# Layer 3's transposed h: TensorE transposes replaced by VectorE block transposes and 16 small DMAs

## The reference, cut to what matters

```python
# layer 0: attention, elu        p = softmax(where(adj > 0.5, leaky(Wh1 + Wh2.T), -9e15), axis=1)
#                                x += elu((p @ h) @ W0)
# layer 1: normalised graph      x += relu(An @ h @ W1 + bias)
# layer 2: plain graph           x += relu((adj @ h) @ W2) * mask
# layer 3 (the one changed):
deg = sum(adj, -1); agg = (adj @ h) / max(deg, 1e-6)
x   = x + relu(concat([h, agg]) @ W3.T)
```

## Time and profile before

| | us |
|---|---|
| median of 3 runs | 2621.51 (2621.48 to 2623.4) |
| the profiled execution's own time | 2621.74 |
| its span, first to last instruction | 2619.9 |
| mean granted TensorE clock | 0.992 of full speed |
| TensorE matmul busy | 2547.1 (97%) |
| VectorE busy | 1823.2 (70%) |
| ScalarE busy | 1408.7 (54%) |
| GpSimd busy | 1185.2 (45%) |

### The profile page before, as it was taken

How to read it: one execution, slowest core, us unless ns; L and a number is a source line. 1 busy time by engine, 2 the same in 40 slices (tenths; PEclk the granted TensorE clock), 3 DMA queues, 4 the chain that set the end, 5 groups by cost and what they waited for, 6 DMA issues and landing times.

```text
span 2619.9 us, 40393 instructions
## 1 busy us (share of the span) xinstructions
PE 2547.1 (97%) x13704; PEld 2205.5 (84%) x13704; DVE 1823.2 (70%) x4251; ACT 1408.7 (54%) x2571; POOL 1185.2 (45%) x1607
## 2 busy tenths in 40 slices
PE   2799999999999999999999999999999999999998
PEld 2688888888888888888888888888888888888886
DVE  6776676676676677677677777777776766766753
ACT  3555555555555555555555555555555555555542
POOL 2544444444444444444444444444444444444431
PEclk8899999999999999999999999999999999999999
DMA  4101111111011011011111111111111111111000
GB/s 140 41 29 49 33 41 49 33 41 49 30 44 49 29 45 49 29 45 46 33 45 41 37 45 41 37 45 35 42 46 33 41 49 33 41 49 33 29 17 25
DMA packets 72844, 109.30 MB, mean 42 GB/s; under 512 B 4288, under 2 KB 37056, under 8 KB 72640
## 3 DMA queue, kind: packets, MB, share of 16 engines
q1 hardware_dynamic: 72640, 106.71, 12.6%
HBM read 73.14 MB, written 33.55 MB: 41 GB/s over the span
## 4 chain that ended last, share of the span: by engine, by line
PE 96%; DVE 1%; issue 1%; ACT 1%; POOL 1%; DMA 0%; SPq 0%; POOLq 0%; ACTq 0%; DVEq 0%
PE O L277 46%; PE T L277 34%; PE X L277 13%; PE X L310 2%; PE X L298 1%; POOL h_lo L747 0%; ACT h L405 0%; DMA act_out<-w_all 0%; POOL xs L712 0%; DVE p_lo L589 0%; DVE scores L522 0%; DVE w_lo L512 0%; DVE t_lo L595 0%; ACT act_out L436 0%; DVE xs L630 0%
## 5 line engine op out<-in xcount | busy, mean ns | idle before, releaser
L747 POOL TENSOR_TENSOR h_lo<-h,h_hi 128x512 fp32r<-128x512 f32 x384 | 503.4, 1333 | 673.1 <-ACT h_hi L411 673.1
L595 DVE TENSOR_TENSOR t_lo<-T,t_hi 128x512 fp32r<-128x512 f32 x512 | 352.5, 690 | 399.1 <-ACT t_hi L417 399.1
L405 ACT ACTIVATE h<-xs,ln_bias,ln_scale 128x512 f32<-128x512 f32 x512 | 396.0, 811 | 391.9 <-POOL ln_bias L741 391.9
L277 PE MATMUL O<-w_hi,t_hi 128*128 128x512 f32 x1536 | 603.2, 393 | 0.0
L277 PE MATMUL O<-w_hi,t_lo 128*128 128x512 f32 x1536 | 598.2, 389 | 0.0
L277 PE MATMUL O<-w_lo,t_hi 128*128 128x512 f32 x1536 | 598.1, 389 | 0.0
L417 ACT CAST t_hi<-T 128x512 fp32r<-128x512 f32 x512 | 298.3, 584 | 257.1 <-PE T L277 257.1
L712 POOL TENSOR_TENSOR xs<-xs,act_out 128x512 f32<-128x512 f32 x128 | 163.7, 1297 | 531.7 <-ACT act_out L439 496.9
L277 PEld LDWEIGHTS O<-w_hi,t_lo 128*128 128x128 f32 x1536 | 288.3, 188 | 60.2
L277 PEld LDWEIGHTS O<-w_hi,t_hi 128*128 128x128 f32 x1536 | 288.5, 188 | 55.9 <-DVE t_lo L595 0.5
L277 PEld LDWEIGHTS O<-w_lo,t_hi 128*128 128x128 f32 x1536 | 288.6, 188 | 55.7
(11 more groups left out here) (92 smaller groups left out, 4991.4 us busy)
## 6 DMA issues: line engine op xcount, KB each, us to landing
xs<-x SPq DMA_DIRECT2D x64, 512.0 KB, 3.6
out<-xs SPq DMA_DIRECT2D x64, 512.0 KB, 2.8
a_raw<-adj_t SPq DMA_DIRECT2D x64, 256.0 KB, 2.7
a_rows<-adj SPq DMA_DIRECT2D x64, 256.0 KB, 2.7
xs<-w_all SPq DMA_DIRECT2D x6, 512.0 KB, 7.3
act_out<-w_all SPq DMA_DIRECT2D x2, 512.0 KB, 6.7
z<-w_all SPq DMA_DIRECT2D x2, 512.0 KB, 6.4
v_rows<-a_vecs SPq DMA_DIRECT2D x1, 512.0 KB, 5.4
```

What stands on the lines that cost most here:

```text
L277: last = nc.tensor.matmul(psum, s, m, start=(start and n == 0 and i == 0), stop=(stop and n == len(pairs) - 1 and i == 2))
L405: nc.scalar.activation(h[:, k.odd, m], xs[:, k.xb, m], ACT.Relu, bias=ln_bias[:, k.quad, m:m + 1], scale=ln_scale[:, k.quad, m:m + 1], acc ...
L595: nc.vector.tensor_tensor(t_lo[:, k.odd, c], T[:, c], t_hi[:, k.odd, c].bitcast(F32), ALU.subtract).then_inc(t_lo_ready, 1)
L747: nc.gpsimd.tensor_tensor(h_lo[:, k.odd, m], h[:, k.odd, m], h_hi[:, k.odd, m].bitcast(F32), ALU.subtract).then_inc(h_lo_ready, 1)
```

## The change

`transpose_h` and its PSUM results go. In slot 0, ahead of `mean_relu`, VectorE waits for layer 3's h and turns it with two transpose instructions (one for each 128 rows), which transpose every 32x32 block within its quadrant of 32 partitions, SBUF to SBUF, into `act_out[:, 1]`. SyncE waits for both, and then issues 16 DMAs, one for each pair of a source and a target quadrant, SBUF to SBUF, ahead of the store of that slot. Each moves 32 partitions x 256 values (32 KB): 1 KB in a row on the source side, eight runs of 32 values (128 bytes) on the target side. The target is the memory of `h[:, 1]` itself, which has been read by then. ScalarE casts it in one instruction to `ht_hi` once all 16 have landed, and VectorE subtracts in one instruction; both now read SBUF where they read PSUM before. ScalarE's next `activate` into `h[:, 1]` waits for that subtraction, `scaled_relu` for the moves.

```diff
+        turned = flat(act_out[:, 1]).rearrange("p (q b n) -> p q b n", q=QUADS, b=FT * NT)
+        turned_tiles = flat(act_out[:, 1]).rearrange("p (q c m n) -> p m c q n", q=QUADS, c=FT, m=NT)
+        h_blocks = h[:].rearrange("p b m (c q f) -> p b m c q f", c=FT, q=QUADS)
+        ht = [flat(h[:, odd]) for odd in range(2)]
+        ht_blocks = [t.rearrange("p (b q n) -> p b q n", q=QUADS, b=FT * NT) for t in ht]
+        MOVES = 16 * QUADS * QUADS
...
# SyncE
+            def move_blocks(k):
+                wait(sp, turned_ready, k.done(L3, NT))
+                for i in range(QUADS):
+                    for o in range(QUADS):
+                        sp.dma_start(ht_blocks[k.odd][QUAD * o:QUAD * o + QUAD, :, i],
+                                     turned[QUAD * i:QUAD * i + QUAD, o]).then_inc(ht_moved, 16)
...
                     load_x(old.g + X_BUFS)
+                if step(j + 3).layer == 3:
+                    move_blocks(step(j + 3))
                 over = step(j - 1)
# TensorE
-                wait(pe, ht_lo_ready, k.done(L3, NT, back=1))          (in spread)
-            def transpose_h(k):
-                wait(pe, h_ready, k.done(ALL, NT))
-                wait(pe, z_ready, k.done(L3, NT, back=4))
-                wait(pe, scores_ready, k.done(L0, NT, back=3))
-                for half in range(2):
-                    for f in range(HALF * half, HALF * half + HALF):
-                        for m in range(NT):
-                            c = (f % HALF) * N + m * P
-                            last = nc.tensor.transpose(X[:, half, c:c + P], h[:, k.odd, m, f * P:f * P + P], ident[:])
-                    last.then_inc(ht_psum_ready, 1)
-                if step(j + 2).layer == 3:
-                    transpose_h(step(j + 2))
# ScalarE
-                wait(act, ht_psum_ready, k.done(L3, NT, back=2))       (in activate)
+                wait(act, ht_lo_ready, k.done(L3, back=2))
             def transposed(k):
                 wait(act, z_psum_ready, k.done(L3, NT, back=4))
-                for half in range(2):
-                    wait(act, ht_psum_ready, k.part(L3, NT, half))
-                    nc.scalar.copy(ht_hi[:, HALF * half:HALF * half + HALF],
-                                   X[:, half].rearrange("p (f n) -> p f n", f=HALF)).then_inc(ht_hi_ready, 1)
+                wait(act, ht_moved, k.done(L3, MOVES))
+                nc.scalar.copy(flat(ht_hi[:]), ht[k.odd]).then_inc(ht_hi_ready, 1)
# VectorE
+            def turn(k):
+                wait(dve, h_ready, k.done(ALL, NT))
+                wait(dve, l1_done, k.done(L1, back=3))
+                for m in range(NT):
+                    nc.vector.transpose(turned_tiles[:, m], h_blocks[:, k.odd, m]).then_inc(turned_ready, 1)
             def transposed(k):
-                for half in range(2):
-                    c = slice(HALF * half, HALF * half + HALF)
-                    wait(dve, ht_hi_ready, k.part(L3, NT, half))
-                    nc.vector.tensor_tensor(ht_lo[:, c], X[:, half].rearrange("p (f n) -> p f n", f=HALF),
-                                            ht_hi[:, c].bitcast(F32), ALU.subtract).then_inc(ht_lo_ready, 1)
+                wait(dve, ht_hi_ready, k.done(L3))
+                nc.vector.tensor_tensor(flat(ht_lo[:]), ht[k.odd], flat(ht_hi[:]).bitcast(F32),
+                                        ALU.subtract).then_inc(ht_lo_ready, 1)
...
+                wait(dve, ht_moved, k.done(L3, MOVES, back=-2))        (in scaled_relu)
...
+                if step(j + 3).layer == 3:
+                    turn(step(j + 3))
                 if step(j - 1).layer == 3:
                     mean_relu(step(j - 1))
```

More of the change, by code:

```diff
@@ L12 @@
 P = 128
+QUAD = 32
+QUADS = P // QUAD
 LAYERS = 4
@@ L85, in sem, with flat @@
             return ctx.enter_context(nc.semaphore(name))
+        def flat(t):
+            return t.rearrange("p m n -> p (m n)")
         w_hi = sb("w_hi", [P, WEIGHTS, FT, F], F32R)
@@ L161, in gnn_kernel @@
         t_ready, o_ready = sem("t_ready"), sem("o_ready")
-        wh_rows_ready, ht_psum_ready, z_psum_ready = sem("wh_rows_ready"), sem("ht_psum_ready"), sem("z_psum_ready")
+        wh_rows_ready, z_psum_ready = sem("wh_rows_ready"), sem("z_psum_ready")
+        turned_ready, ht_moved = sem("turned_ready"), sem("ht_moved")
         stats_ready, mv_ready, neg_mean_ready, var_ready, rstd_ready, scale_ready, ln_ready = (
@@ L196, in tiles @@
             return dram[g].rearrange("(m p) f -> p m f", p=P)
-        def flat(t):
-            return t.rearrange("p m n -> p (m n)")
         def flat_blocks(t):
@@ L293, in spread @@
                 wait(pe, wh_ready, k.done(L0, DOTS))
-                wait(pe, ht_lo_ready, k.done(L3, NT, back=1))
                 wait(pe, scores_ready, k.done(L0, NT, back=4))
@@ L341, in project_first @@
                     wait(pe, w_lo_ready, 2 * WEIGHT_ORDER.index(4) + 2)
-                wait(pe, ht_lo_ready, k.done(L3, NT))
+                wait(pe, ht_lo_ready, k.done(L3))
                 for n in range(NT):
@@ L401, in activate @@
                 wait(act, wh_ready, k.done(L0, DOTS, back=2))
-                wait(act, ht_psum_ready, k.done(L3, NT, back=2))
+                wait(act, ht_lo_ready, k.done(L3, back=2))
                 for m in range(NT):
@@ L614, in scaled_relu @@
                 wait(dve, deg_rsqrt_ready, k.done(L0, back=SPACING))
+                wait(dve, ht_moved, k.done(L3, MOVES, back=-2))
                 for n in range(NT):
```

## The result

The changed kernel takes 2653.58 us (median of 4 runs, 2651.91 to 2655.87) against 2621.49 us: a ratio of 1.0122, 95% interval 1.0105 to 1.014. It is 32 us slower; I had forecast 27 us faster. The profiled execution has a span of 2654.1 us against 2619.9, 34.1 us more before rounding.

What follows compares the result with a forecast made beforehand. TensorE was taken to bound the kernel: -53.1 us for 61 graphs without transposes, +3.5, +10.2 and +10.3 for exposed ends, +2 for the clock, -27.1 on 2621.7, gave 2594.5 us; range 2580 to 2730.

Steps and rivals of the forecast that it cites:

- What bounds, and what is removed: TensorE bounds the steady part; removing its eight transposes of h saves 0.87 us in each of 61 graphs.
- Step 1: Layer 3's h is ready at 1316.88; VectorE waits 1.2 us for it at the head of its slot.
- Step 2: Two block transposes of 128x512 on VectorE take 0.65 us each, done at 1318.2.
- Step 3: SyncE, idle there, issues 16 DMAs 0.53 us apart; the last issue starts at 1326.2.
- rival B: ht_lo misses its place beside GpSimd, waits for the second h_lo, 0.7 us late per graph: 2639 us; chance 0.17.
- Step 4: The last DMA lands at 1328.9, with 13 ns estimated for a 128-byte piece, 57 ns at the upper end.
- rival A: Small DMA pieces are slower than the issues and set the pace: 2713 us at 45 ns a piece; chance 0.27.
- Step 8: TensorE wants ht_lo at 1332.3, leaving 0.6 us of cover; nothing is added to the period.
- Step 7: VectorE's ht_lo, 1.22 us with two SBUF sources, waits for GpSimd's h_lo until 1330.5 and ends at 1331.7.
- Step 6: VectorE's slot 0 moves by 2.5 us, but T is still free in time for TensorE, with 2.4 us of cover.
- The ends: New path exposed in the first graph, +3.5 us, and the last two, +10.2 and +10.3, plus 2 for the clock.
- My sign of being wrong: The prediction is wrong if TensorE waits for ht_lo in the steady part.

Runs made afterwards that it cites:

- experiment 2: Changed kernel, 16 moves with 1 KB target rows: 2637.5 us; or a quarter of the size in 128-byte pieces: 2638.8 us.
- experiment 7: Changed kernel with 12 moves, ScalarE copying four blocks, graph 0 and the last three by TensorE transposes: 2568.13 us, 0.9794 to the kernel before.
- experiments 1: Changed kernel with only 8 of the 16 moves, half of the transposed h left out: 2586.1 us, ratio 0.9866 to the kernel before.
- experiment 3: Kernel before, with the two block transposes and their wait added on VectorE, result unread: 2633.5 us, ratio 1.005.

## Why the prediction was wrong, step by step

- **What bounds, and what is removed: right.** With the landing in time, the period is 38.66; removed are 0.91 us a graph where I had 0.87.
- **Step 1, h and its wait: right.** h is ready 9.3 us after the attention gather's end, as before; VectorE waits 1.16 us for it in the graph below.
- **Step 2, the turn: right.** I took 0.65 us each. From VectorE's timeline, and SyncE's behind it:

```profile
1322.78 1.31 DVE L607 STREAM_TRANSPOSE act_out<-h 128x512 f32<-128x512 f32 x2 [1.16 <-ACT h L411]
1324.01 1.37 DVE L637 SCALAR_TENSOR_TENSOR z<-O,deg_recip,z 128x512 f32<-128x512 f32 x2
```

```profile
1324.11 10.88 SPq L259 DMA_DIRECT2D h<-act_out  x16
1335.03 0.60 SPq L279 DMA_DIRECT2D out<-xs  x1
```

- **Step 3, the pace of the issues: this is the step that failed.** I took 0.53 us from the ten issues at the start, and argued in rival B that an idle queue would be quicker still. It is 0.653 us at best: sixteen back to back take 10.40 us where nothing disturbs them, 10.88 above, and up to 12.2 in other graphs, where one or two issues last up to 2.05 us (1.09 us in the chain above). Fifteen gaps at 0.12 us more are 1.8 us. Even the store behind them costs 0.60 us where a lone issue costs 0.37. Why a DMA right behind another costs more here than at the start, no run shows; experiment 2 shows that the pieces and the bytes account for 0.02 us of the 0.12 at most.
- **Step 4, the landing: half right.** The last DMA lands 1.9 us after the start of its issue, 0.8 us less than I took from a 256 KB load. The price of a piece, which carried rival A and the upper end of my range, never mattered. (Rival A's lateness at 40 ns should be 0.54 us by its own terms, not 0.44.)
- **Steps 3 and 4 together**, from the first issue to the start of the cast: 10.65 us forecast; 11.78 measured at least, 12.3 in the mean of the steady graphs. Step 8 had left 0.6 us of cover.
- **Step 7, two SBUF sources beside GpSimd: the mechanism right, and it costs part of the loss.** One graph without a held-up issue, from the timelines of SyncE, ScalarE, GpSimd, VectorE and TensorE:

```profile
1363.42 10.40 SPq L259 DMA_DIRECT2D h<-act_out  x16
1375.21 1.05 ACT L428 CAST ht_hi<-h 128x1024 fp32r<-128x1024 f32 x1 [1.61 <-DMA h<-act_out]
1374.02 2.72 POOL L759 TENSOR_TENSOR h_lo<-h,h_hi 128x512 fp32r<-128x512 f32 x2
1376.30 1.53 DVE L611 TENSOR_TENSOR ht_lo<-h,ht_hi 128x1024 fp32r<-128x1024 f32 x1 [1.95 <-ACT ht_hi L428]
1377.88 0.50 PE L297 MATMUL T<-w_hi,ht_hi 128*128 128x512 f32 x1 [0.20 <-DVE ht_lo L611]
```

  `ht_lo` is asked for at 1376.30, GpSimd's pair ends at 1376.74, and `ht_lo` takes 0.30 us longer than the 1.23 it takes alone. The same happens in 23 of the steady graphs (1.27 to 1.58 us), and these have the periods of 39.13 to 39.20. It is a floor: however much earlier `ht_lo` comes while the second `h_lo` runs, it ends at the same time, and experiment 2 has the same 39.13. Where issues are held up, `ht_lo` comes after the pair and takes 1.23. In experiment 7 it gets in between the two: its median is 2242 ns, and GpSimd's pair takes 3.72 us for the 2.56 it takes undisturbed (at 1307.33 in the changed kernel), longer by about the one subtraction. So the two take turns. By the Trainium skill, "SBUF — State Buffer", Who interferes with whom, the loser blocks and isn't slowed down in proportion; the trace agrees: slowed by 1316/418 = 3.1 for the 0.44 us that are left of the pair, `ht_lo` would have taken the same 1.53 us here, but in experiment 2, with 0.90 us left, 1.84 us and not 1.99.
- **What a steady graph loses.** The path is 1.13 us longer than forecast at the least, and 0.6 us of that was covered. An undisturbed graph is 0.47 us late (39.13 - 38.66); 0.30 of these are the wait for GpSimd, so by an estimate from this graph's rows the issues alone would make it 0.17 us late. Held-up issues add the rest: 0.9 us late in the mean, and 0.91 was the gain.
- **Step 6 and what stands behind `ht_lo`: right for the steady part.** T came free in time and nothing behind SyncE's issues was late: in experiments 1 and 3, which have the turn and its wait too, no steady period is longer for them.
- **The ends: the mechanism right, the size short.** Graph 0: +4.3 for +3.5. The last two graphs: 11.3 + 13.0 us between first products where I had 10.2 + 10.3 and 2 for the clock; the path is 1.1 us longer each time (11.78 for 10.65), and the second has 1.7 us of the clock (0.23 x 7.6). TensorE had waited 13.9 us for `ht_lo`, and then worked for 7.6 us at a granted clock of 0.77 (the last number but two; busy time by engine stands ahead of it, DMA share and GB/s behind), a mean of its two levels of 1.2 and 2.4 GHz:

```profile
2596.40:2604.00 7.60, 7.57 (x26) 6.19 (x27) 0.69 (x1) 0.81 (x2) 0.00 (x0) 0.77 0.00 0
```

  The third graph from the end, +5.1 us, I hadn't seen at all. The turn's place in VectorE's order comes into the path there (experiment 3 has 4.6 of the 5.1 us), and so does the clock, 0.77 between 2545 and 2560 us. How much falls to each, no run separates.
- **The rivals.** What happened is B, in part: the landing came more than 0.4 us late, and `ht_lo` ran into the second `h_lo`. I gave it only 0.17, because I thought the issues of an idle queue quicker than 0.53 us. B gave 2639 us and the runs 2654: it lacked the held-up issues, the longer paths at the end and the third graph from the end. A fell with experiment 2. The range, 2580 to 2730, held the time by luck: its upper part was there for A's pieces, which cost nothing, and the likeliest value lay on the wrong side of no change. My sign of being wrong, TensorE waiting for `ht_lo` in the steady part, came true.

## What to carry to other kernels

Work taken off the bounding engine is a gain only by the cover that its substitute has left, so compute that cover in tenths of a microsecond, and take the price of a chain of small DMAs from as close a pattern as there is: here a misjudged 0.12 us per issue came to 1.8 us a graph, against a gain of 0.9 and a cover of 0.6. Look also at what a late piece runs into: `ht_lo` came 0.4 us before the end of a GpSimd instruction, and had to wait for it. Another order of the two on GpSimd's side was not tried. Count the issues before the bytes: blocks that stay in their quadrant need no DMA, and a second queue with idle time takes half of the moves. What is hidden behind other graphs' work is not hidden in the first and last ones; keep the short path there (it was worth 27 us here, 2595 against 2568).

## What the runs showed of the hardware

- DMAs issued back to back on SyncE's queue from one SBUF tensor to another cost 0.65 us each at 256 pieces of 128 bytes, 0.64 at 64 such pieces and 0.63 in 1 KB rows: nearly nothing hangs on the shape. A lone issue costs 0.37 us.
- GpSimd issues the same DMA in 0.59 us, at the same time as SyncE and without slowing it.
- A transpose of 32x32 blocks on VectorE, 128x512 fp32, SBUF to SBUF, takes 0.69 us listed and 0.62 us from one to the next, as VectorE's statistics of the same width do (0.68 us).
- Four ScalarE copies of 32 partitions x 256 values take 401 ns each, as long as casts of 128 x 256 (0.40 us): with three quarters of the lanes idle the time is the same.
- A VectorE subtraction of 128x1024 with both sources in SBUF takes 1.23 us alone, 1.53 where it is asked for 0.44 us before the end of a GpSimd subtraction with two SBUF sources, 1.99 where it is 0.90 us before, and 2.24 between the two instructions of a GpSimd pair, which takes 3.72 us then for 2.56.
- In 37 of the 59 steady graphs of the changed kernel the issues are held up, by 0.3 to 1.8 us together. No experiment was made on it, but the trace shows something that comes with it. The instruction queue moves one 16 KB packet every 23 us or so (count, MB and share of 16 engines, over the whole run):

```profile
q8 instruction: 107, 1.75, 0.3%
```

  32 of its packets start while moves are being issued, and 30 of these start between 0.4 us before and 0.2 us after the start of an issue that is held up (over 0.75 us to the next one). Only 45 of 960 issues are held up at all. So most hold-ups come together with a load of instructions. No run changed that load, so it stays a coincidence in time and is not shown as the cause.
